# Two layers with attention and eight experts: one sequence's tokens sent to their two experts only

## What is computed

```python
logits = xf @ Wr + br                                  # 8 experts
topk_w, topk_idx = top_k(logits, 2)                    # 2 of 8 for each token
gate = sum(one_hot(topk_idx, 8) * softmax(topk_w)[..., None], axis=1)
h = relu(einsum('th,ehf->etf', xf, W1) + b1)           # 128 -> 256, every expert
y = einsum('etf,efh->eth', h, W2) + b2                 # 256 -> 128
out = einsum('te,eth->th', gate, y)
```

## Time and profile before

| | |
|---|---|
| median of 3 runs | 1236.21 us |
| time of the profiled execution | 1233.06 us |
| its span from first to last instruction | 1231.1 us |
| PE matmul busy | 1108.1 us, 90% |
| VectorE busy | 883.3 us, 72% |
| ScalarE busy | 753.3 us, 61% |
| GpSimd busy | 274.9 us, 22% |
| moved by DMA | 57.70 MB, 47 GB/s on the mean |

### The profile page before, as it was taken

One profiled execution on the slowest core, in us unless ns is written; L12 is line 12 of the kernel. 1 busy time (PEld: TensorE's weight loads), 2 busy tenths in 40 slices (PEclk: granted clock), 3 DMA queues, 4 the chain that ended last, 5 costly groups with the idle time before them and its releaser, 6 DMA issues. The chain is left out here.

```text
span 1231.1 us, 24956 instructions
## 1 busy us (share of the span) xinstructions
PE 1108.1 (90%) x8797; PEld 606.1 (49%) x8872; DVE 883.3 (72%) x2136; ACT 753.3 (61%) x1505; POOL 274.9 (22%) x800
## 2 busy tenths in 40 slices
PE   5899998899999989999988998888888878899996
PEld 3466676656777745666555632212112212127775
DVE  3788767783445478888767888988999898914444
ACT  4377656567434426776656667677888767874332
POOL 8134322332002113433333310111101010100000
PEclk9899999999999999999999999999999999999998
DMA  3444343110001600344221311000211100000000
GB/s 87 122 112 110 93 96 89 47 36 8 1 1 27 157 20 31 81 100 101 66 74 31 64 35 30 22 11 15 40 35 34 29 11 17 7 1 1 10 9 18
DMA packets 40058, 57.70 MB, mean 47 GB/s; under 512 B 9495, under 2 KB 15079, under 8 KB 39679
## 3 DMA queue, kind: packets, MB, share of 16 engines
q1 hardware_dynamic: 39934, 56.11, 18.5%
HBM read 30.81 MB, written 24.64 MB: 45 GB/s over the span
## 5 line engine op out<-in xcount | busy, mean ns | idle before, releaser
L838 ACT ACTIVATE probs<-bank 128x512 f32<-128x512 f32 x1088 | 574.7, 603 | 268.9 <-PE bank L1206 267.4
L937 DVE TENSOR_REDUCE tile_max<-bank 128x1 f32<-128x512 f32 (+3 forms) x1152 | 612.0, 593 | 51.4 <-PE bank L1191 47.2
L1191 PE MATMUL bank<-qk 125*128 125x128 bf16 (+2 forms) x1664 | 389.2, 311 | 83.8 <-DVE tile_max L937 65.4
L1206 PE MATMUL bank<-qk 128*128 128x128 bf16 (+4 forms) x1608 | 362.6, 305 | 3.9 <-ACT probs L838 3.6
L1235 PE MATMUL bank<-probs,v_head 128*32 128x512 f32 (+3 forms) x3328 | 304.6, 455 | 0.1
L1191 PEld LDWEIGHTS bank<-qk 125*128 125x128 bf16 (+1 forms) x1664 | 133.6, 97 | 329.1 <-DVE tile_max L937 249.5
L1113 DVE SCALAR_TENSOR_TENSOR acc<-bank,gate,acc 128x128 f32<-128x128 f32 x256 | 72.0, 344 | 143.0 <-PE bank L1364 143.0
L1235 PEld LDWEIGHTS bank<-probs,v_head 128*32 128x32 f32 x3328 | 140.2, 109 | 50.2 <-issue 28.0
L1206 PEld LDWEIGHTS bank<-qk 128*128 128x128 bf16 (+1 forms) x1664 | 134.3, 96 | 52.7 <-ACT probs L838 16.8
L858 ACT ACTIVATE probs<-bank,sb_b 128x512 f32<-128x512 f32 x128 | 80.9, 683 | 123.3 <-PE bank L1353 123.3
L931 DVE TENSOR_REDUCE tile_max<-bank 128x4 f32<-128x512 f32 x128 | 87.4, 688 | 87.5 <-PE bank L1191 87.2
(11 more groups left out here) (130 smaller groups left out, 653.1 us busy)
## 6 DMA issues: line engine op xcount, KB each, us to landing
qk<-qk_parts SPq DMA_DIRECT2D x160, 144.0 KB
qk_parts<-q_parts SPq DMA_DIRECT2D x48, 192.0 KB, 2.4
qk_parts<-k_parts SPq DMA_DIRECT2D x48, 192.0 KB, 3.1
qk_parts<-q_parts SPq DMA_DIRECT2D x24, 96.0 KB, 2.3
qk_parts<-k_parts SPq DMA_DIRECT2D x24, 96.0 KB, 2.9
sb_w<-in_w SPq DMA_DIRECT2D x8, 256.0 KB, 3.8
sb_w<-in_w SPq DMA_DIRECT2D x2, 1024.0 KB, 5.3
qk<-neg_rows SPq DMA_DIRECT2D x96, 6.0 KB
```

The source lines that it names most:

```text
L838: nc.scalar.activation(probs[:, hd.probs_place(c), :], S2[i % len(S2)][:], ACT.Exp, scale=hd.a.scale).then_inc(sem("probs"), 1)
L937: ins = nc.vector.tensor_reduce(tile_max[:, hd.slot, t, which:which + 1], s1[:, at:at + P * count], AX.X, ALU.max)
L1191: ins = mm(s1[:, at:at + P * count], qk[hd.query_rows, hd.place, 0, P * t:P * (t + 1)], qk[hd.query_rows, hd.place, 1, P * k0:P * (k0 + co ...
L1206: ins = mm(s2[:, at:at + P * count], qk[hd.key_rows, hd.place, 1, P * j:P * (j + 1)], qk[hd.key_rows, hd.place, 0, P * q0:P * (q0 + count) ...
```

## The change

Sequence 0's 1024 tokens have 2048 pairs of token and expert. The kernel after counts, on the chip, how many pairs each expert has, gives each expert whole blocks of 128 slots, and so fills at most 23 blocks (`BLOCKS`); it always computes 23. Sequence 1 is computed as before. A stage has 6 block units (four blocks each, three in the last) and 16 dense units, 22 in place of 32.

- **During the heads**: `ranks` (PE: nine small bf16 matmuls; DVE copies), `blocks`, `slots` and `biases` (DVE: some 25 small instructions, each waiting for the one before), then 16 `scatter` steps, each one indirect DMA on POOL of 128 rows of 512 bytes to `x_blocks` in DRAM. In layer 1 the tokens to be sent are first transposed back (`mtok`, two times four transposes). The two `x_blocks` tensors are cleared by one DMA each of 1.5 MB on SP, behind heads 2 and 4.
- **SP, for each block**: reads the expert's number from SBUF into a register and loads 128 KB of first weights by it, and the same again for 128 KB of second weights. The first two block units are loaded after the last `load_max` of the heads, then their x; unit m+2's first weights after `up(m)`, its second weights after `down(m)`. The weights go into the SBUF place of the other layer's weights.
- **Six places in front** of the first unit (`IN_FRONT`) hold the end of sequence 1's attention and the first two `gx` steps (PE transposes four blocks of x through `SHARED`, DVE copies them out), with no unit beside them; the other four `gx` lie in units 0 to 3. `turn_sums` and `normalise` come before them.
- **Outputs**: DVE copies a block unit's `Y` to SBUF, SP stores it to DRAM. After all six stores, POOL issues 16 indirect gathers, eight for each chunk of sequence 0, and DVE adds them with the routing weights (`combine`, before unit 10 and in unit 12). `gateT` and `gb` of sequence 0, before in the heads, are now in the expert stage. The layer sum, norm, and next q, k, v of chunks 0 and 1 follow their `combine`.

```diff
+TOP = 2
+BLOCKS = (TOP * S + E * (P - 1)) // P
+BLOCK_UNITS = -(-BLOCKS // TPC)
+UNITS = BLOCK_UNITS + CB * E
+IN_FRONT = 6
...
+first = at_unit(0, -1, 0)
+put_attention_out(0, 1, first, (0, 1, 2, 3, 4, 5, 6, 7, 9, 10))
+for m, i in enumerate((4, 5, 6, 8, 10, 12)):
+    put(later(first, i), ("gx", 0, m))
+put_routing(0, 1, first, (11, 12, 13, 14, 15))
+put_gate_sums(0, 1, first, (16, 17, 19, 20))
+put_gate_sums(0, 0, first, (13, 14, 15, 18))
+for c, i in enumerate((26, 31)):
+    put(later(first, 19), ("gather", 0, c))
+    put(later(first, i), ("combine", 0, c))
+    put_next_qkv(c, later(first, i + 1))
+    put(later(first, i + 8), ("bias", 1, c))
...
+first = at_unit(1, -1, 0)
+for m, i in enumerate((0, 1, 6, 8, 10, 12)):
+    put(later(first, i), ("gx", 1, m))
+put_attention_out(2, 1, first, (2, 3, 4, 5, 6))
...
+            def load_w1(f, m):
+                for j in blocks_of(m):
+                    e = nc.sync.value_load(expert_i[0:1, j:j + 1], min_val=0, max_val=E - 1)
+                    sp.dma_start(block_weights(f)[0][:, TPC * (m % 2) + j % TPC, :],
+                                 inp[f"w1_{f}"][0][:, bass.ds(e, 1), :].rearrange("p a f -> p (a f)")
+                                 ).then_inc(sem(f"w1_in{m % 2}"), 16)
...
+            def first_blocks(f):
+                sp.wait_ge(sem("experts_known"), f + 1)
+                ge(sp, "y_ps", UNITS * f)
+                for m in range(2):
+                    load_w1(f, m)
+                for m in range(2):
+                    load_w2(f, m)
+                sp.wait_ge(sem("scattered"), 16 * TOP * TB * (f + 1))
+                for m in range(2):
+                    load_x(f, m)
+
+            def blocks(f):
+                for m in range(BLOCK_UNITS):
+                    n = len(blocks_of(m))
+                    if m + 2 < BLOCK_UNITS:
+                        taken(sp, "gx", f, m)
+                        load_x(f, m + 2)
+                        sp.wait_ge(sem("hid_ps"), UNITS * f + m + 1)
+                        load_w1(f, m + 2)
+                        sp.wait_ge(sem("y_ps"), UNITS * f + m + 1)
+                        load_w2(f, m + 2)
+                    sp.wait_ge(sem("y_taken"), UNITS * f + m + 1)
+                    sp.dma_start(y_blocks[f].rearrange("(j p) d -> p j d", p=P)[:, TPC * m:TPC * m + n, :],
+                                 y_out[:, m % 2, 0:P * n].rearrange("p (j d) -> p j d", d=D)
+                                 ).then_inc(sem(f"y_stored{m % 2}"), 16)
...
+            def gather(f, c):
+
+                pool.wait_ge(sem("pv"), BATCHES[RUNS[f].stop])
+                for m in range(2):
+                    pool.wait_ge(sem(f"y_stored{m}"), 16 * BLOCK_UNITS // 2 * (f + 1))
+                for i in (0, 1):
+                    for t in range(TPC * c, TPC * (c + 1)):
+                        at = TB * i + t
+                        nc.gpsimd.indirect_dma_start(
+                            yg[:, at, :], None, y_blocks[f],
+                            bass.IndirectOffsetOnAxis(ap=places[:, at:at + 1], axis=0)).then_inc(sem(f"gathered{c}"), 16)
...
                 def up(m):
-                    c, e = m // E, m % E
                     ge(pe, "hid", FB * (UNITS * f + m - 1))
-                    for fb in range(FB):
-                        ins = mm(bank[2 * (m % 2) + fb][:], w_sb[f"w1_{f}"][:, e, P * fb:P * (fb + 1)],
-                                 xT[:, tokens(c)], start=True, stop=True)
+                    if m < BLOCK_UNITS:
+                        taken(pe, "gx", f, m)
+                        pe.wait_ge(sem(f"w1_in{m % 2}"), 16 * blocks_in(f, m))
+                        w1 = block_weights(f)[0]
+                        for fb in range(FB):
+                            for j in blocks_of(m):
+                                of = slice(P * (j % TPC), P * (j % TPC + 1))
+                                ins = mm(bank[2 * (m % 2) + fb][:, of],
+                                         w1[:, TPC * (m % 2) + j % TPC, P * fb:P * (fb + 1)], xgT[m % 2][:, of],
+                                         start=True, stop=True)
...
                 loaded(pe, f"ffn{f}")
                 pe.wait_ge(sem("max_taken"), CHUNKS[RUNS[f].stop])
+                turn_sums(last)
+                for i in range(IN_FRONT):
+                    between(at_unit(f, -1, i))
                 up(0)
-                turn_sums(last)
```

More of the change, by code:

```diff
@@ L203, in put_attention_out, with put_routing, put_gate_sums, put_places_of_tokens @@
     return at[9]
[L206 to L209, removed]
-        put(later(place, i), step)
+def put_routing(f, b, place, at):
+    for i, step in zip(at, ("logits", "route_top", "route_exp", "route_weights", "route_gate")):
+        put(later(place, i), (step, f, b))
+def put_gate_sums(f, b, place, at=range(4)):
+    for i, step in zip(at, [(kind, f, c) for c in BY_SEQUENCE[b] for kind in ("gateT", "gb")]):
+        put(later(place, i), step)
+def put_places_of_tokens(f, place, at, each):
+    for i, step in zip(at, ("ranks", "blocks", "slots", "biases")):
+        put(later(place, i), (step, f))
+    for i in range(TOP * TB):
+        put(later(place, at[2] + 1 + i // each), ("scatter", f, i))
 def put_qkv(L, c, place, every=1):
@@ L545, in _ @@
                 load_weight(*piece)
+            first_blocks(0)
+            blocks(0)
             for four in range(len(FOURS)):
@@ L725, in _ @@
                 add_quarters(GROUP[run.stop - 1])
-                for m in range(UNITS):
-                    for half in range(2):
-                        between(at_unit(f, m, half))
+                between(later(at_unit(f, -1, 0), -1))
+                for place in units_places(f):
+                    between(place)
         @block.scalar
@@ new lines, in combine @@
+            def combine(f, c):
+                dve.wait_ge(sem(f"gathered{c}"), 16 * TOP * TPC * (f + 1))
+                taken(dve, "gb", f, c)
+                for i in range(TOP):
+                    for t in range(TPC * c, TPC * (c + 1)):
+                        ins = nc.vector.scalar_tensor_tensor(acc[:, t, :], yg[:, TB * i + t, :], small[:, 1 + i, t:t + 1],
+                                                             acc[:, t, :], ALU.mult, ALU.add)
+                    if i == 0:
+                        link(ins)
+                ins.then_inc(sem("combined"), 1)
@@ L1101, in experts @@
             def experts(f, last):
+                normalise(last)
+                for i in range(IN_FRONT):
+                    between(at_unit(f, -1, i))
+                dve.wait_ge(sem("out"), last + 1)
                 for m in range(UNITS):
-                    c, e = m // E, m % E
                     at = UNITS * f + m
```

281 lines of the change are left out of this document (237 added, 44 removed).

## The result

The kernel after took 1287.16 us (median of 4 runs, 1283.47 to 1290.43), the kernel before 1234.32 us beside it (4 runs, 1231.8 to 1237.85): ratio 1.0425, 95% interval 1.0383 to 1.0467. It is slower by 53 us; the forecast was 1243, and the measurement lies 7 us above the end of its range, 1208 to 1280. All figures leave out one execution of the kernel before, beside e13 to e15, that took 1329.94 us at a mean granted clock of 0.84. PE's matmuls are busy for 1098.4 us (1108.1 before): the work that was taken out barely shows, since what is left runs in part at the low clock, and new steps such as `ranks` and `gx` came in.

A forecast was written before the change was run, and what follows sets the result against it. The prediction took PE to bound the kernel before, with SP's issues bounding the new block stage. Layer 0 +1.3, layer 1 +0.2, stores +4.5, heads +2.8 and clearings +1 gave +9.8 on 1233.06: 1243 us, range 1208 to 1280.

The forecast's parts named there:

- the block stage: Six block units in each layer's expert stage: SP's issues set the pace, 10.8 us a unit, 47.5 us in all.
- c: SP's time per block and weight, register load plus DMA issue: 1.2 us, with ends 0.6 and 2.5.
- Issues under 1.0 apart: Sign in the block stage: SP's weight issues this close would prove the forecast wrong to the fast side.
- 0.8 in down(5): Low granted clock at the end of the block stage: 0.8 us, counted once within the block stage's sum.
- front of layer 0: Steps ahead of layer 0's first unit: SP's weights and x come last, up(0) 16.3 us late, 17.3 with the clock.
- front of layer 1: Steps ahead of layer 1's first unit: SP's lateness is added because gx precedes aT, 14.8 us late.
- stores: SP's 24 stores behind layer 0's experts, partly uncovered by the shorter dense part: +4.5 us, from 0 to 9.
- heads and last sums: Some 25 linked DVE instructions a layer in the heads, less savings: +2.8 us together, from -3 to +9.
- clearings: Two 1.5 MB clearings in the heads, 7.4 us each ahead of the next maxima: +1 us, from 0 to 8.
- Dense parts: Sixteen dense units a layer at 3.5 us, 54.3 us, plus steps of 11.8 (layer 0) or 3.0 (layer 1) and 2 clock.
- the cheap register load: Rival in SP's block loads: register load cheap or overlapped, c 0.8, -32 us, 1211 us; chance 0.34.
- POOL held by gathers: Rival in the dense units: gathers past 1.24 us each delay root; at 1.9 us, +21, 1264 us; chance 0.16.

The follow-up runs named there:

- e13: Kernel after, unchanged, timed again in a later set of runs: 1314.19 us, ratio 1.0644 to the kernel before.
- e15: Kernel after with the four edits and all 64 indirect DMAs (scatters and gathers) left out: 1234.3 us.
- e1: Kernel after with SP issuing x of unit m+3 ahead of the second weights of unit m+2: 1274.3 us.
- e3: Kernel after without register loads, each block's weights loaded by a constant expert number: 1272.3 us.
- e6: Kernel after with bf16 matmuls that nobody reads filling PE's waits in the front and ahead of the later gx: 1265.3 us.
- e17: Kernel after with the four edits and the 32 gathers left out, scatters kept: 1236.4 us.
- e4: Kernel after without the 32 indirect scatters, blocks computing on cleared rows: 1277.6 us.
- e11: Kernel after with the four edits and DVE doing biases twice, six more instructions a layer: 1269.1 us.
- e5: Kernel after with 12 of the 24 stores behind layer 0 moved behind heads 32 to 37: 1278.6 us.
- the four edits: Kernel after with x loaded earlier, clearings in eight pieces, 12 of 24 stores moved later, each expert number read once for both weights: 1239.7, 1263.23, 1264.28 us.
- e7: Kernel after with the four edits, first execution: 1239.7 us, 3 above the kernel before.
- e10: Kernel after with the four edits and the weights of block units 2 to 5 not loaded: 1245.99 us.
- e12: Kernel after with the four edits, same text as e7, timed in six runs: 1263.23 us, ratio 1.0240 to the kernel before.
- e14: Kernel after with the four edits, timed a third time beside e13: 1264.28 us, ratio 1.0244 to the kernel before.
- e16: Kernel after with the four edits, POOL issuing each scatter only when the one before has landed: 1263.1 us.

## Why the prediction was wrong

**The step that failed is the block stage**, "SP's own time for a unit is 8c + 2 x 0.6 = 10.8 us". It took SP for a queue that issues without a stop. But its entries wait for PE, and PE waits for one of them: x of unit m+2 is issued behind the second weights of the unit before, which wait for a `down`, which stands on PE behind a `gx`, which waits for x. The costs of single instructions were weighed, the loop was never walked through. Its period is 12.4 us; e1 takes x out of it and gets 9.8, e3 shortens SP's issues by 3.8 us and the unit by only 1.6. c itself was too high, 0.92 in the blocks (1.0 to 1.07 in the front) for 1.2. With 0.92 the prediction's own rule (9.2 us for each 0.1) gives 1217 us, 70 below the measurement: two errors of opposite sign lay in one term, and its time looked better than its reasoning. The block stage alone comes to 39.1 us by the prediction's sum with 0.92, for 55.3 and 56.2 measured. Issues under 1.0 apart had been named as the sign of a faster kernel; they came, and the kernel was slower. The Trainium skill, "DMA: Bandwidth & Descriptors", Latency and other measured facts, gives about 600 ns as the floor of such a load; here e3 shows 0.48 us, and the measurement decides.

**The clock in the loop.** "0.8 in down(5)" and 1.7 in `up(0)` were counted once. `down(5)` ran at the upper level, and PE was busy for 57 to 68% of the blocks, not under half; but the `down` of units 1, 2 and 3 ran low in part or whole (3.08 to 3.62 for 1.95 us), and it stands in the loop. e6 shows what both layers lose by it in the fronts and blocks, 18.6 us.

Term by term, on the span:

| term | predicted | measured |
|---|---|---|
| front of layer 0 | 17.3 | 17.3 |
| block stage of layer 0 | 47.5 | 55.3 |
| dense part of layer 0 | 68.1 | 71.3 |
| front of layer 1 | 14.8 | 17.8 |
| block stage of layer 1 | 47.5 | 56.2 |
| dense part of layer 1 | 59.3 | 59.2 |
| stores | +4.5 | +5.3 |
| heads and last sums | +2.8 | +13.5, and 4.4 by the clock |
| clearings | +1 | +7.8 |
| gathers | 0 | 0 |
| behind layer 1's last `down`; the first head behind layer 0 | 0 | +1.7, +0.8 |

The span came out 47.7 us above the forecast of +9.8. 16.5 of these are the block stages', 10.7 the heads', 6.8 the clearings', 6.1 the fronts' and dense parts', 4.4 the clock's in the heads, and 3.3 lie in the last rows and the stores.

- **Front of layer 0**: the number is right by luck, its reason only in part. I had SP last; in the trace the first `gx` waits for DVE's `x_plus`, the end of attention at the low clock (`proj` 2.05, not 1.05), and SP's x had landed.
- **Front of layer 1**: SP was the last, as predicted, and a little quicker (`gx` 5.4 us behind the sums, not 6.5). From there to `up(0)` it took 12.4 us for 8.3: I had given this front no low clock.
- **Dense parts**: units at 3.50 and, in layer 1, the whole to 0.1 us. Layer 0 lost 2.1 us of its 3.2 in two waits of PE for DVE, 0.53 for the norm and 1.55 for `qk`'s result to be taken out behind a `combine`. Both are in e17 too, so they aren't POOL's or the gathers'.
- **Clearings**: 1.5 MB do not only take their 7.4 us, they stand ahead of the weight load and the next head's q and k on the same queues, so the head behind waits. The low end of the cover was taken, and 8 stood in the range.
- **Heads**: I took 5.3 us less savings. Layer 1 alone costs 7.0, of which e4 leaves 6.1 without scatters; e11 shows 1.3 to 1.9 times such an instruction's own length there. That DVE's 25 instructions are the 6.1 us fits this, but no run took them out. In layer 0 scatters and steps cost 6.5; e4 and e15 put 4.2 to 5.6 of it to the scatters, which I had at 0, and leave 0.7 to 2.1 for the other steps, which I had at 3.8. One wait of PE there is for a mask, which stands behind scatters on POOL ([0.68 <-POOL probs L877] above).
- **Stores** and **gathers** came out as worked out: the gap is 6.70 us (1.45 before), e5 brings it to 1.22; 16 gathers take 1.25 us each, and PE is busy for 20.00 of 20 us beside them.
- **Rivals**: the cheap register load was nearly right in c (0.92 for 0.8) and wrong in what follows from it. POOL held by gathers didn't occur in the first measurement: behind the last one POOL idles 1.68 us until DVE's `mean_var` is there. In e13 the gathers do cost time, though not by POOL's length but by stopping the other engines.

**What the change could give**: the four edits bring the kernel after from 53 above the kernel before to about 3 above it in e7, one execution, and to 2.4% above it where it was timed, with the stops. e15 and e17 equal the kernel before with parts of the work left out. e10 is 17 us below e12. Were that so beside e7, it would give some 1222 us (an estimate from these three; the block stages' 10.3 and 9.3 us give 1220), 1% below the kernel before; this was not run, and needs weights that are not fetched for each block. No complete version beat the kernel before.

## What to carry to other kernels

Before pricing a queue by its issue time, write down for each entry what it waits for and who waits for it; if that closes a ring that is longer than the queue's own time for a round (here 12.4 us for 8.6), the ring's length is the period. Work that is taken from a full engine is worth its time only if the engine stays full: behind waits it ran at the low clock, and the rest got dearer (18.6 us here). A large transfer with a far deadline still delays the small ones behind it with a near one, so cut it into pieces and put them where loads are sparse.

## What the runs showed of the hardware

- **Indirect DMAs can stop other engines.** One kernel text gave 1239.7 us in one set and 1263.2 and 1264.3 in two others, with DVE, ACT and PE stopped together: DVE and ACT wait 2.0 and 2.4 us in heads with scatters, and 16 gathers cost 9 to 11.5 us. A program without indirect DMAs didn't change between the sets (1231 to 1238 us). What decides whether a set has the stops was not found; e7, without them, and e14, with them, have the same chip number on record. e16, meant to test whether it takes several transfers in flight, ran in a set without stops, so that is open.
- An issue of a 128 KB weight DMA from SP takes 0.44 us (four in 1.75, e3), a register load ahead of it 0.48, and where a DMA of another kind went before, the next issue begins 0.77 us after its end, load included (357.93 + 0.43 to 359.13 in e1).
- An indirect DMA of 128 rows of 512 bytes keeps POOL for 0.94 us, and gathers start 1.25 us apart; a scatter keeps it for 0.95 to 1.24 us, and scatters start 1.26 to 1.33 us apart where nothing lies between.
- Indirect DMAs lengthen POOL's last instruction, a drain behind its last `root`: 1.15 us without any (e15 and the kernel before), 3.78 with 32 (e4, e17), 6.39 with 64. With 6.39 the program ends 1.7 us later behind its last `down` (10.9 us for 9.2 to 9.3); with 3.78 it doesn't.
